# Rows of unit 8, projection pieces and tiles at other places in TensorE's order, and one weight split moved from GpSimd to VectorE

## The reference

```python
x = x + _layernorm(_L0_attn_ref(_layernorm(x), q_w, k_w, v_w, o_w, q_b, k_b, v_b, o_b))
x = x + _layernorm(_L0_ffn_ref(_layernorm(x), w_gate_up, w_down))

def _L0_attn_ref(h, ...):           # 16 heads of 32, causal
    q, k, v = proj(q_w, q_b), proj(k_w, k_b), proj(v_w, v_b)
    scores = where(ki > qi, -inf, q @ k.T / sqrt(32))
    return (softmax(scores) @ v) @ o_w.T + o_b

def _L0_ffn_ref(h, w_gate_up, w_down):   # inner width 2048
    gate, up = split(h @ w_gate_up.T)
    return (silu(gate) * up) @ w_down.T
```

## Time and profile before

| | us |
|---|---|
| median of 3 runs | 997.32 (995.51 to 997.4) |
| the profiled execution, its own time | 994.97 |
| its span, first to last instruction | 993.1 |
| PE busy | 963.2 (97%) |
| DVE busy | 704.8 (71%) |
| POOL busy | 675.9 (68%) |
| ACT busy | 430.1 (43%) |
| mean granted clock of PE | 0.998 |

### The profile page before, as it was taken

How to read it: one execution, slowest core, us unless ns; L and a number is a source line. 1 busy time by engine, 2 the same in 40 slices (tenths; PEclk the granted TensorE clock), 3 DMA queues, 4 the chain that set the end, 5 groups by cost and what they waited for, 6 DMA issues and landing times.

```text
span 993.1 us, 15626 instructions
## 1 busy us (share of the span) xinstructions
PE 963.2 (97%) x5604; PEld 744.2 (75%) x5604; DVE 704.8 (71%) x1394; ACT 430.1 (43%) x761; POOL 675.9 (68%) x494
## 2 busy tenths in 40 slices
PE   7999999999999999998999999999999999999996
PEld 5776667676776677654878888888888888888885
DVE  7467777776886788788786777775827877777722
ACT  4566555454125555465344333322543443333242
POOL 5338787799328999982569766634886668666272
PEclk9999999999999999999999999999999999999999
DMA  7512333333412333231342211114232312211143
GB/s 248 158 46 76 79 81 82 94 88 85 133 53 67 86 86 82 65 92 35 137 138 75 95 65 64 64 43 148 85 117 96 107 64 85 85 64 64 34 151 135
DMA packets 49182, 90.70 MB, mean 91 GB/s; under 512 B 10448, under 2 KB 10960, under 8 KB 48848
## 3 DMA queue, kind: packets, MB, share of 16 engines
q1 hardware_dynamic: 48018, 88.66, 29.1%
q10 hardware_dynamic: 1086, 1.03, 0.4%
...
## 4 chain that ended last, share of the span: by engine, by line
PE 82%; DVE 12%; ACT 2%; issue 2%; DMA 1%; POOL 0%; SPq 0%; ACTq 0%; DVEq 0%; POOLq 0%
PE ps L1823 20%; PE ps L1825 20%; PE ps L1824 20%; PE ps L1921 7%; PE ps L1955 6%; PE ps L1895 6%; DVE ps L1448 2%; PE ps L1970 2%; PE ps L1929 1%; DVE xt_lo L1425 1%; DVE stats L1616 1%; DVE attn L1490 1%; DVE stats L1621 1%; DVE p_sum L1403 1%; DMA x_in<-x 1%
## 5 line engine op out<-in xcount | busy, mean ns | idle before, releaser
L1448 DVE CUSTOM_DVE_ANT_0 ps<-ps,mask_q 128x384 f32<-128x384 f32 (+7 forms) x256 | 190.0, 779 | 61.4 <-PE ps L1895 58.9
L1921 PE MATMUL ps<-q_stack,k_stack 98*128 98x512 f32 (+3 forms) x384 | 115.2, 378 | 3.5 <-DMA q_stack<-x_in 2.0
L1895 PE MATMUL ps<-k_stack,q_stack 96*128 96x512 f32 (+3 forms) x384 | 106.4, 359 | 0.7 <-DVE v L1439 0.6
L822 POOL TENSOR_TENSOR dn_lo<-dn_raw,dn_hi 128x512 fp32r<-128x512 f32 x48 | 66.3, 1383 | 42.8 <-ACT dn_hi L1209 42.8
L1895 PEld LDWEIGHTS ps<-k_stack,q_stack 96*128 96x128 f32 x384 | 66.1, 190 | 25.8 <-DVE m_full L1448 11.3
L1921 PEld LDWEIGHTS ps<-q_stack,k_stack 98*128 98x128 f32 x384 | 61.9, 189 | 28.7 <-issue 5.8
L867 POOL TENSOR_TENSOR gu_lo<-s_raw,gu_hi 128x1024 fp32r<-128x1024 f32 x27 | 64.9, 2402 | 22.7 <-ACT gu_hi L1280 22.7
L1303 ACT ACTIVATE silu<-ps 128x512 f32<-128x512 f32 x27 | 16.2, 599 | 141.5 <-DVE ps L1714 141.5
L1081 ACT ACTIVATE p_own<-ps 128x512 f32<-128x512 f32 x112 | 60.9, 598 | 31.0 <-PE ps L1921 19.5
L1081 ACT ACTIVATE x_in<-ps 128x512 f32<-128x512 f32 x112 | 60.9, 598 | 30.0 <-PE ps L1921 19.0
L863 POOL TENSOR_TENSOR a_lo<-gu_raw,a_hi 128x512 fp32r<-128x512 f32 x27 | 35.9, 1330 | 52.2 <-ACT a_hi L1273 52.0
...
## 6 DMA issues: line engine op xcount, KB each, us to landing
...
k_stack<-st_hi SPq DMA_DIRECT2D x128, 64.0 KB, 2.1
...
```

The lines of the kernel that those rows point to most:

```text
L822: nc.gpsimd.tensor_tensor(dn_lo[:, s], dn_raw[:, s], dn_hi[:, s].bitcast(F32), ALU.subtract).then_inc(dn_split, 1)
L1448: nc.vector.tensor_tensor_reduce(out=scores, in0=scores, in1=mask_q[:, SEQ - (t + 1) * P:], scale=1.0, scalar=MASKED, op0=ALU.add, op1=ALU ...
L1895: last = nc.tensor.matmul(bank[:, 0:width], q_stack[0:QK_ROWS, s, h, t * P:(t + 1) * P], k_stack[0:QK_ROWS, s, h, half * CH:half * CH + wi ...
L1921: last = nc.tensor.matmul(bank[:, at_col:at_col + n * P], k_stack[0:ROWS, s, h, kt * P:(kt + 1) * P], q_stack[0:ROWS, s, h, t * P:(t + n) ...
```

## The change

Five edits:

1. **Rows of unit 8** are made at the end of unit 7: `negated` and `max_rows` on DVE follow unit 7's last maximum (ahead of V0's bias), the small matmul on PE stands between the late values of unit 7 and V0, and ACT issues the DMA ahead of `copy_acc`. The table of uses moves two uses accordingly. SP waits for that DMA before it loads into `x_in`.
2. **Projection pieces.** The four pieces of unit 10's first chunk leave the start of unit 8: k=0 follows V2, k=1 and 2 follow T4, k=3 follows V6 (`BETWEEN`). ACT's load of the Exp table with its dummy activation moves from behind T7's high part to ahead of T6's.
3. **Tiles in units 1 to 4.** The transposes of the two tiles move from ahead of the early values to between rounds (0, 1, 3) and rounds (2, 4). In all units up to 13 the early values now wait for their exponentials in two parts.
4. **End stage, chunk 2.** The first two pieces of its gate half come ahead of T4 (after O7); the other 18 matmuls still follow T4.
5. **Chunk 4's low weights** are made by DVE right after h of chunk 1 instead of by POOL. POOL's first `pair_sums` wait for `h_ready` 2, and `pair_lows(5)` for chunk 4's low part.

```diff
@@ tables @@
-AFTER_TILE = {("O", 3): (1, WHOLE), ("T", 4): (2, WHOLE), ("T", 5): (3, ((0, 0, KT),)), ("T", 6): (3, ((1, 0, KT // 2),)),
+AFTER_TILE = {("O", 3): (1, WHOLE), ("O", 7): (2, ((0, 0, KT // 2),)), ("T", 4): (2, ((0, KT // 2, KT), (1, 0, KT))), ("T", 5): (3, ((0, 0, KT),)), ("T", 6): (3, ((1, 0, KT // 2),)),
+BETWEEN = {("V", 2): (0,), ("T", 4): (1, 2), ("V", 6): (3,)}
@@ def row_uses(g) @@
+    if g == UNITS:
+        return 0
@@ def use_body(g) @@
-            use += SUM_BANKS + len(MID)
+            use += NCH + SUM_BANKS + len(MID)
@@ def use_of_rows(g) @@
-    return use_body(g)
+    return USE_MID - NCH if g == UNITS else use_body(g)
@@ SP, residual @@
+                if b + 1 < BATCH:
+                    sp.wait_ge(m_loaded, DMA * (UNITS + 1))
@@ POOL @@
                     if b + 1 == BATCH and t == 7:
+                        pool.wait_ge(h_ready, 2)
                         pair_sums(STD)
...
-            gu_rest(EARLY_CHUNKS)
             dn_rest(2)
             dn_rest(3)
+            pool.wait_ge(gu_split, EARLY_CHUNKS + 1)
             pair_lows(STD)
@@ ACT, body(g) @@
-                if g + 1 < ALL_UNITS:
+                if g not in (UNITS, ALL_UNITS - 1):
                     load_maxima(g)
...
+                if g + 1 == UNITS:
+                    load_maxima(UNITS)
                 if g % UNITS == UNITS - 1:
                     copy_acc(g)
@@ ACT, residual @@
+                    if b + 1 < BATCH and t == TT:
+                        act.wait_ge(std_ready, TT + 1 + (b + 1) * (TT + 1))
+                        nc.scalar.activation(unused[:, :], eps[:, :], ACT.Exp)
@@ ACT, loop over the batches @@
-                nc.scalar.activation(unused[:, :], eps[:, :], ACT.Exp)
+                if b == 0:
+                    nc.scalar.activation(unused[:, :], eps[:, :], ACT.Exp)
@@ DVE, body(g) @@
-                negated(g)
+                if g != UNITS:
+                    negated(g)
...
-                max_rows(g)
+                if g != UNITS:
+                    max_rows(g)
@@ DVE, residual @@
                         hidden(1)
+                        vec.wait_ge(gu_hi_done, EARLY_CHUNKS + 1)
+                        nc.vector.tensor_tensor(gu_lo[:, 0], gu_raw[:, 0], gu_hi[:, 0].bitcast(F32), ALU.subtract).then_inc(gu_split, 1)
@@ DVE, after the units of a batch @@
+                if b + 1 < BATCH:
+                    negated(UNITS)
+                    max_rows(UNITS)
@@ PE, body(g) @@
-                if g:
+                if g and g != UNITS:
                     project_next(0, 0, 1, 2)
-                if projected:
+                if projected and g != UNITS:
                     transpose_maxima(g)
...
-                project_next(0, 3)
+                if g != UNITS:
+                    project_next(0, 3)
...
+                values(g, EARLY_VALUES[:3])
                 for t in REST_TILES.get(g, ()):
                     transpose_rest(t, use_of_rest(g, t))
-                values(g, EARLY_VALUES)
+                values(g, EARLY_VALUES[3:])
@@ PE, stage between the batches @@
+            def pieces_of_unit_10(kind, t):
+                for k in BETWEEN.get((kind, t), ()):
+                    project(UNITS + 2, 0, (k,))
...
-                    residual(b, MID[:BEFORE_SUMS], lambda kind, t: None)
+                    transpose_maxima(UNITS)
+                    residual(b, MID[:BEFORE_SUMS], pieces_of_unit_10)
...
-                    residual(b, MID[BEFORE_SUMS:], lambda kind, t: None)
+                    residual(b, MID[BEFORE_SUMS:], pieces_of_unit_10)
```

## The result

| | before | changed |
|---|---|---|
| median of 5 runs, us | 997.4 (995.51 to 999.08) | 991.45 (990.65 to 993.55) |
| ratio, 95% interval | | 0.9944 (0.9924 to 0.9963) |
| profiled execution, us | 994.97 (span 993.1) | 993.07 (span 991.2) |

A forecast was written before the change was run, and what follows sets the result against it. PE (TensorE), busy 97% of the span, bounds the kernel; only its idle time could be saved. Savings of 2.1 + 2.0 + 0.8 = 4.9 us gave 992.4 us against the median 997.32, range 989.4 to 995.6.

The forecast's parts named there:

- A: Stage between the batches through unit 8's start: moved rows, projection pieces and table load save 2.1 us (0.8 to 3.0).
- B: Units 1 to 4: tile transposes amid the early values save 0.5 us a unit, 2.0 in all (0.0 to 2.4).
- C: End stage: POOL kept away from h_lo brings the second down projection 0.8 us forward (0 to 1.2).
- My bank argument: Unit 8's start: four PSUM banks, freed by T6, V7 and T7, set M1 at 295.5, scores(8, 0) at 296.3.
- The drain of 1.38 us: Table load on ACT: skill's extra cost per switch, ending T6's high part 1.4 us later; forecast followed the trace instead.
- The cover of 0.2 us: Units 1 to 4: low parts end at about 98.3, M13 needs their banks at 98.5.
- Split 0: End stage: splitting chunk 2 around T4 only moves PE's idle time to T6 and T7; worth 0.
- 1 fell: Units 1 to 4: moved tiles give nothing, low parts late for M13, maxima late for rows; 994.4 us, chance 0.12.
- 2 fell: Between the batches: late banks or rows stalling V0 leave a saving of 0.8 us, not 2.1; 993.7, chance 0.14.
- 3 fell: End stage: POOL's pair sums hold up DVE's `gu_lo`, chunk 4 starts 1.8 us late; 994.2 us, chance 0.08.
- 4 named the right mechanism: End stage, T6 and T7: holes drop PE's clock to 1.2 GHz; slower, 1002.4 with 10 us of work; chance 0.03.
- a sign of being wrong: Middle of the program: a granted clock under 1.0 there would show the forecast wrong.

The follow-up runs named there:

- run 9: The changed kernel itself, unaltered, measured again beside variants and the kernel before: median 990.61 us, ratio 0.9934.
- run 3: Kernel before with only the tile transposes of units 1 to 4 moved amid the early values: 995.38 us, ratio 0.9997.
- run 5: Changed kernel with the Exp table load back at its old place, behind T7's high part: 992.12 us, ratio 0.9927.
- run 10: Changed kernel with the table load at its old place and seven small filler matmuls in unit 8's start: 990.79 us, ratio 0.9935.
- run 11: Changed kernel with the two tiles of units 1 to 4 moved behind all five early values: 994.18 us, ratio 0.9967.
- run 7: Changed kernel without the split of chunk 2, its first pieces back behind T4: 992.11 us, ratio 0.9931.
- run 8: Changed kernel with POOL making chunk 4's low weights again and not held back: 993.16 us, ratio 0.9942.
- run 4: Kernel before with only the end-stage changes (chunk 2 split, chunk 4's low weights on DVE, POOL held): 994.61 us, ratio 0.9987.
- run 1: Kernel before with only unit 8's rows, the projection pieces and the table load moved: 993.61 us, ratio 0.9982.

## Why the prediction was right, and where it was off

The forecast of 4.9 us against the profiled execution stands: A 2.56 (forecast 2.1), B 1.3 to 1.47 (forecast 2.0), C 0.70 to 0.74 (forecast 0.8), in all 4.6 to 4.8 where no spell lies. That the sum is so close is partly luck: A was 0.46 too low and B 0.6 too high.

The measured difference of medians, 5.95 (6.8 beside run 9), is larger. The fastest executions differ by 4.9 (995.51 and 990.65) and 4.4 (994.23 and 989.83 beside run 9), near the sum; the medians of before lie further above its fastest executions than those of the changed kernel do. One reason can be named. The second h_lo of before can meet POOL's `gu_lo` (run 3), and then edit 5 is worth 2.8 us instead of 0.7; the profile that the forecast started from had no such meeting. How much of the remaining 1 to 2 us it explains is open, since single executions were not profiled. Two executions of before with a mean clock of 0.999, at 997.45 and 998.31, are later by 1.7 and 2.3 us than the slowest at 0.998 beside them (995.75 and 995.97), as the meeting would make them; that is not shown.

**A, 0.46 too low, right in its places.** Edit 1 alone is 1.68 of the 2.56, edit 2 the other 0.9: the pieces gain 1.3 (2.98 less 1.68) and the moved load takes 0.4 back. The rows cost PE nothing (I charged 0.2), and the four pieces in the holes of O0, T5 and T6 cost nothing, as forecast; T6 is still 0.2 late. Scores (8,0) were forecast 2.5 us earlier than before and came 2.68 earlier counted from T7; scores (8,1) 2.0 and came 2.30 (2.40 without the spell); the rest came before the rows of unit 9. My bank argument held: high part, low part and V7's bias set M1, M2 and scores (8,0), and the maxima behind the last low part set M5 and scores (8,1). What I did not draw from it was that the load was the step to leave out: I listed it as ahead of T6's high part and never priced it at its old place. There it makes the first exponentials wait (PE waits 0.28 us for one of them, run 5); moved, it costs 0.4 us more (run 10).

**The table load.** It took 1.28 us at 291.10 and the activation behind it started at 292.39. The drain of 1.38 us in the Trainium skill (ScalarE: Activation LUTs, What ACT_TABLE_LOAD costs) is not seen at this place either, and the saving of 0.7 that followed from it is excluded by the 2.56.

**B, 0.6 too high.** The term was 0.5 a unit, from 0.45 of idle plus 0.15 that the issue showed less 0.1 for switches. It measured 0.33 to 0.37. If the hole is worth its idle 0.45 us, the two switches cost about 0.1 together, and what was wrong is the 0.15 added for the issue; the runs do not separate the two. The cover of 0.2 us ahead of M13 held; run 11 shows what lies behind it.

**C, right in sum and terms.** Split 0 (run 7), first projection 0.4 and second 0.8 (0.40 and 0.72), T6 and T7 idle 0.57 and 0.74 for a forecast 0.7 and 0.9. Its upper bound of 1.2 was too low: where POOL's `gu_lo` meets the second h_lo, as in runs 3 and 8, the edit saves 2.8, and I had not seen that it could.

**Rivals.** 1 fell (B is there). 2 fell: A is 2.56, though a spell left only 0.15 of it in the first profile, which read alone would have spoken for this rival. 3 fell: `gu_lo` on DVE took 1.22 us, begun 0.16 before POOL's first pair sum; it was POOL that was held up (1.65 us against 0.74 for the next). The blocking that the rival rests on is there, though. Subtract each operation's time alone and what is left is the rest of the other's: POOL's sum, 1.65 from 521.39, ends 0.6 after DVE's `gu_lo` does at 522.45; DVE's h_lo in run 8, 2.74 from 521.04, ends 0.54 after POOL's `gu_lo` (523.24), for 0.74 and 0.69 alone. So the rule of the Trainium skill (SBUF — State Buffer, Who interferes with whom), that the second to issue waits until the first has finished, agrees with these rows within 0.15 us. I had argued against the rival with the h_lo at 519.55 that lost only 0.4 us: beside a short operation that is what full blocking costs. POOL's sum, 0.90 from 519.20, ended at 520.10, and the h_lo 0.55 later. What decided was who came first, and how long the other's operation is. 4 named the right mechanism at the wrong place: the clock did fall in the middle of the program, which I had listed as a sign of being wrong, but behind unit 8's start and around the last units' start, not at T6 and T7 of the end stage, which are at full clock in every trace; and it falls in runs of the kernel before's order too (runs 3 and 4). It costs 0.9 to 2.4 us a spell, not the 7 to 10 of the rival.

**What stays open.** What sets off a spell. Those behind the start of the program begin 0.1 to 2.6 us after PE had waited 0.85 to 1.83 us, but for the one at 298 in run 5, which has only waits of 0.26 and 0.28 ahead of it. The same instructions with the same waits stay at full clock in other traces: the start of unit 8 in runs 1, 7, 8 and 11, against the changed kernel and run 9. Run 10's holes are the best filled, its profile has no spell, and its times still spread over 2.7 us.
